# Gathers ahead of the histogram's end without waits, and a different mix of gathers and scatters

## The reference

```python
h = relu(layernorm(x))                        # over each row's 128 numbers
deg = segment_sum(1, src); deg_inv = rsqrt(deg) where deg > 0, else 0
norm = deg_inv[src] * deg_inv[dst]
msg[e] = alpha[type[e]] * norm[e] * sum_b comps[type[e], b] * (h[dst[e]] @ bases[b])
out = x + segment_sum(msg, src)               # 4 bases of 128 x 128
```

## Time and profile before

| | us |
|---|---|
| median of 3 runs | 767.62 (767.0 to 768.07) |
| profiled execution, time | 762.65 |
| profiled execution, span | 760.8 |
| POOL busy | 548.0 |
| DVE busy | 595.4 |
| PE busy | 565.7 |
| ACT busy | 368.6 |

### The profile page before, as it was taken

One profiled execution on the slowest core, in us unless ns is written; L12 is line 12 of the kernel. 1 busy time (PEld: TensorE's weight loads), 2 busy tenths in 40 slices (PEclk: granted clock), 3 DMA queues, 4 the chain that ended last, 5 costly groups with the idle time before them and its releaser, 6 DMA issues. The chain is left out here.

```text
span 760.8 us, 13653 instructions
## 1 busy us (share of the span) xinstructions
PE 565.7 (74%) x3922; PEld 396.5 (52%) x3922; DVE 595.4 (78%) x2624; ACT 368.6 (48%) x1494; POOL 548.0 (72%) x404
## 2 busy tenths in 40 slices
PE   1999995566576886659769778777889669788860
PEld 0766654344354664446556556555666446554430
DVE  4999995578577897749879899869998869896630
ACT  0144346245343565455646565644566546465530
POOL 1788886344237777877888888888888778777875
PEclk9999997988798999999989999989999989999995
DMA  3899989989944545344444445435444534444332
GB/s 116 293 353 350 321 306 336 315 276 349 317 131 91 94 98 103 54 85 89 95 81 98 95 80 96 96 54 117 76 79 94 112 63 96 78 71 73 35 36 24
DMA packets 56527, 108.89 MB, mean 143 GB/s; under 512 B 9291, under 2 KB 48216, under 8 KB 55636
## 3 DMA queue, kind: packets, MB, share of 16 engines
q0 software_dynamic: 34496, 25.72, 25.0%
q1 hardware_dynamic: 5372, 55.14, 20.0%
q10 hardware_dynamic: 16584, 27.16, 11.6%
HBM read 94.89 MB, written 64.61 MB: 210 GB/s over the span
## 5 line engine op out<-in xcount | busy, mean ns | idle before, releaser
L389 POOL DMA_INDIRECT out_dram<-acc,scatter_idx x196 | 313.2, 1598 | 97.2 <-issue 43.7
L368 POOL DMA_INDIRECT rows<-in_x_dram,dst_i x196 | 232.8, 1188 | 107.5 <-issue 39.0
L723 PE MATMUL pst<-table_bits,turned_hot 128*128 128x198 f16 x1568 | 177.0, 261 | 79.4 <-DVE masked L476 63.4
L742 PE MATMUL pst<-bases_sb,h_turned 128*128 128x512 f32 x392 | 211.6, 623 | 0.0
L723 PEld LDWEIGHTS pst<-table_bits,turned_hot 128*128 128x128 f16 x1568 | 143.1, 103 | 106.4 <-issue 50.6
L513 DVE SCALAR_TENSOR_TENSOR part_sum<-pst,coef,part_sum 128x128 f32<-128x128 f32 x392 | 115.9, 344 | 104.7 <-ACT part_sum L636 100.2
L750 PEld LDWEIGHTS pst<-rows,same 128*128 128x128 f32 x392 | 71.3, 197 | 184.0 <-issue 160.5
L476 DVE SCALAR_TENSOR_TENSOR masked<-iota_h,lo,pst 128x198 f32<-128x198 f16 x392 | 141.7, 416 | 15.9 <-PE pst L723 8.7
L636 ACT ACTIVATE part_sum<-pst,coef 128x128 f32<-128x128 f32 x196 | 71.1, 363 | 154.2 <-PE pst L742 114.3
L750 PE MATMUL pst<-rows,same 128*128 128x128 f32 x392 | 83.5, 296 | 72.8 <-ACT acc L646 69.9
L646 ACT ACTIVATE acc<-pst,sum_scale 128x128 f32<-128x128 f32 x196 | 71.5, 365 | 81.9 <-DMA out_dram<-acc,scatter_idx 56.3
(11 more groups left out here) (71 smaller groups left out, 413.6 us busy)
## 6 DMA issues: line engine op xcount, KB each, us to landing
out_dram<-in_x_dram SPq DMA_DIRECT2D x50, 1000.0 KB
src_row<-src_rows ACTq DMA_DIRECT2D x25, 512.0 KB
edge_row<-edge_rows ACTq DMA_DIRECT2D x45, 256.0 KB
rows<-in_x_dram,dst_i POOLq DMA_INDIRECT x196
out_dram<-acc,scatter_idx POOLq DMA_INDIRECT x196
rows<-edge_rows ACTq DMA_DIRECT2D x10, 175.0 KB
edge_row<-edge_rows SPq DMA_DIRECT2D x4, 256.0 KB
src_row<-src_rows SPq DMA_DIRECT2D x2, 512.0 KB
```

What stands on the lines that cost most here:

```text
L368: pool.indirect_dma_start(row(t), None, x, bass.IndirectOffsetOnAxis(ap=dst_i[:, t:t + 1], axis=0)) \
L389: pool.indirect_dma_start(out, bass.IndirectOffsetOnAxis(ap=scatter_idx[:, t:t + 1], axis=0), acc[:, t % ACC_RING, :], None, compute_op=AL ...
L723: last = pe.matmul(pst[:, LOOK + t % 2, k * LO:(k + 1) * LO], turned_hot[:, g % 2, c, k * W + j * P:k * W + (j + 1) * P], table[:, c * LO: ...
L742: pe.matmul(pst[:, PRODUCT + t % 4, :], h_turned[:, g % 2, j, :], bases_sb[:].rearrange("d b f -> d (b f)"), start=True, stop=True).then_i ...
```

## The change

`GATHER_RING` and its wait go; each of the 49 groups has a semaphore of its own. Of `pace` only the part for t below 56 stays. `FIRST_GATHERS` rises from 88 to 128, and in the scatter loop `gathers_until` gives one gather for two scatters, where it gave seven for ten. `stats_until` is not edited, but it calls `gathers_until`.

```diff
-    GATHER_RING = 8
-    HIST_GATHERS, LOOK_GATHERS, FIRST_GATHERS = 56, 64, 88
+    HIST_GATHERS, FIRST_GATHERS = 56, 128
     def gathers_until(t):
-        return min(TILES, FIRST_GATHERS + (7 * t + 9) // 10)
+        return min(TILES, FIRST_GATHERS + t // 2)
...
-        row_gathered = [sem(f"row_gathered{r}") for r in range(GATHER_RING)]
+        row_gathered = [sem(f"row_gathered{g}") for g in range(GROUPS)]
...
             def pace(t):
                 if 0 < t < HIST_GATHERS:
                     pool.wait_ge(hot_used, t * TILES // HIST_GATHERS)
-                elif HIST_GATHERS <= t < LOOK_GATHERS:
-                    pool.wait_ge(look_ps, ...)
-                elif LOOK_GATHERS <= t < FIRST_GATHERS:
-                    pool.wait_ge(product_ready, (t - LOOK_GATHERS) // 2 + 1)
             def gather(t):
                 g = t // GROUP
-                if t % GROUP == 0 and g >= GATHER_RING:
-                    pool.wait_ge(row_squared, g - GATHER_RING + 1)
                 pace(t)
...
-                    .then_inc(row_gathered[g % GATHER_RING], 16)
+                    .then_inc(row_gathered[g], 16)
...
             def stats(g):
-                act.wait_ge(row_gathered[g % GATHER_RING], 16 * GROUP * (g // GATHER_RING + 1))
+                act.wait_ge(row_gathered[g], 16 * GROUP)
```

More of the change, by code:

```diff
@@ L353, in pace @@
                     pool.wait_ge(hot_used, t * TILES // HIST_GATHERS)
-                elif HIST_GATHERS <= t < LOOK_GATHERS:
-                    pool.wait_ge(look_ps, (t - HIST_GATHERS + 1) * FIRST_LOOK * GROUP // (LOOK_GATHERS - HIST_GATHERS))
-                elif LOOK_GATHERS <= t < FIRST_GATHERS:
-                    pool.wait_ge(product_ready, (t - LOOK_GATHERS) // 2 + 1)
             def gather(t):
                 g = t // GROUP
-                if t % GROUP == 0 and g >= GATHER_RING:
-                    pool.wait_ge(row_squared, g - GATHER_RING + 1)
                 pace(t)
```

## The result

| | before | after |
|---|---|---|
| median, us | 767.31 (764.4 to 768.07, 4 runs) | 831.64 (825.72 to 833.66, 4 runs) |
| ratio | | 1.083 [1.077, 1.090] |
| profiled execution, time / span | 762.65 / 760.8 | 832.76 / 830.9 |

A forecast was written before the change was run, and what follows sets the result against it. POOL was taken to bound the loop, DVE next. Step 11 at 329, 29 steps of 10.7 us to 639 and 92 to the end give a 731.5 us span; with 1.85 and 5 added, 738, range 717 to 758.

The forecast's parts named there:

- No engine is made to wait.: Early gathers before the scatter loop: behind them is queued only the first scatter, which waits for the copies anyway; no cost.
- The end of the gathers: Early gathers on POOL: 72 at 1.27 us, 91 us in all, ending at 205 us, before the copies end.
- Rival C: Early gathers slow at 1.94 us each, ending at 254 us, where the scatters then start: 751 us; chance 0.16 with its like.
- D: Steps 1 to 4: look-up loads starve behind POOL's gathers, +32 us, 778 us in all, slower than before; chance 0.08.
- What they cost the copies: Stretch with DMA full: 40 more gathers, 2.6 MB, delay the copies by 8 us, bounds 0 and 19.
- S: Start of the scatter loop, set by the end of the copies: moves from 219.7 to 228 us.
- Steps 5 to 10: Two groups of statistics a step, DVE covering about 3 of 6.2 us: 13.4 us a step, 80 us by DVE's sum.
- Steps 11 to 40: Scatter loop: 29 steps of 10.7 us, 310 us, from 329 to 639, where 665.81 was.
- B: The forecast itself: DVE and the chain round it set the steps, 738 us, own range 730 to 746; chance 0.42.
- A: POOL still sets every step of the loop: -43 us, 725 us; chance 0.27.
- Step 40 to the end: Last stretch, bound by POOL's scatters as before: 92 us, where it was 95.

The follow-up runs named there:

- x9: The changed kernel a third time, unedited, in a job on chip 10: 830.05 us, 1.080 of the kernel before.
- x10: Changed kernel with gathers 56 to 127 waiting for look-ups and products, and ACT's statistics on the schedule of before: 746.23 us, 0.970 of the kernel before.
- x5: The changed kernel again, unedited, in another job on another chip: 743.58 us, 0.976 of the kernel before.
- x4: Changed kernel with 2 of the 50 copies of x to out, the other 48 left out: 733.9 us in one run.
- x14: Changed kernel without 48 of its 50 table copies, as x4, on another chip: 730.52 us.
- x17: Changed kernel without 48 of its 50 table copies, as x4, once more: 736.07 us in one run.
- x3: Changed kernel plus a watcher: ACT follows each of the first twelve look-ups with a small operation on DVE's semaphore: 736.0 us in one run.
- x12: Changed kernel with ACT's twelve watching operations, as x3, on another chip: 738.87 us, 0.969 of the kernel before.
- x16: Changed kernel with ACT's twelve watching operations, as x3, once more: 746.75 us in one run.
- x8: Changed kernel with ACT's statistics kept on the schedule of before: 727.71 us, 0.957 of the kernel before.
- x6: x3 again, the changed kernel with ACT's twelve watching operations: 745.26 us, 0.978 of the kernel before.
- x13: Changed kernel with three awaited small memsets on POOL between two of the early gathers: 765.04 us, 1.004 of the kernel before.
- x18: Changed kernel with three awaited small memsets between two early gathers, as x13, once more: 764.59 us in one run.
- x1: Changed kernel with waits back for gathers 56 to 127, on look-ups and then products: 741.46 us, 0.972 of the kernel before.

## Why the prediction was wrong, point by point

- **"No engine is made to wait."** This is the step that failed; the stretch before step 0, in which it put the cost at nothing, took 91.5 us more. I asked only what is queued behind the gathers on POOL. The waits that went also kept POOL's descriptors from running in one piece beside the first look-ups, and in two of six jobs the look-ups came up to 43 us late beside this piece. x9 and x10 show that the waits decide it on chip 10; for the first job that is taken over from there, and 10.9 of its 91.5 us were lost earlier, beside gathers that still waited for the histogram. The 1.26 us of a gather were right; what it did to others wasn't asked.
- **The end of the gathers**, forecast 205, came at 215.8 (215.5 in x5). The price was right, the start wrong: the sum counts 72 gathers from 113.9, where the kernel before is at its 50th; its 57th starts at 123.30.
- **Rival C and D** looked at the right stretch for other reasons. C's gathers beside DVE weren't slow: 0.95 us with DVE at work in x5 too. D's mechanism is there, but small. Steps 0 to 5 went from 105.6 us to 118.9 in x5, where I had allowed 2 us more, and D 32. In that stretch of x5 DVE waits for look-up loads (total, times, longest):

```profile
DVE turned_hot L463 <- DMA edge_row<-edge_rows: 9.5, 4, 3.2
```

  In the kernel before these waits are 0.4 us. In x4, x14 and x17, without copies, there are none and the steps take 104 to 107 us; in x3, x12 and x16, with them, 110 to 115. After and x9 reach these steps when the copies are over: no such wait, 107.2 and 105.6.
- **What they cost the copies**: 8 us, S at 228. In x5 the first scatter stands at 220.49, against 219.73 before: at most 1 us. In the stalled run SyncE's queue is done sooner than before:

```profile
23.06 177.63 SPq L309 DMA_DIRECT2D out_dram<-in_x_dram  x49
```

  at 200.7 against 212.9.
- **Steps 5 to 10**, 80 us by DVE's sum and 77 in the forecast, took 92.4 (91.7, 90.2 in x5, x9). The mechanism was named, two groups of statistics in one piece; its size was wrong. I took DVE's cover as 3 us of each 6.2, so that DVE waits 3 us a step; it waited 31.1 / 6 = 5.2. A step took 15.4 us; with at most one group, 11.7 (x8).
- **Steps 11 to 40**, forecast 310, took 304.0, 304.4 and 304.3: 10.5 us a step in place of 10.7. DVE was busy 284 of the 304 us, POOL 236 without its gaps. POOL by line, 435 to 740 us, against the earlier trace rows:

```profile
L382 POOL DMA_INDIRECT out_dram<-acc,scatter_idx x116 | 186.5, 1608 | 54.7 <-issue 27.5 <-DMA out_dram<-acc,scatter_idx 14.5 <-ACT acc L639 12.6
L361 POOL DMA_INDIRECT rows<-in_x_dram,dst_i x48 | 50.9, 1060 | 14.6 <-issue 13.1 <-ACT acc L639 0.9 <-DMA out_dram<-acc,scatter_idx 0.6
```

  The prices of a scatter and a gather haven't moved (1608 and 1060 ns), and POOL waits 13.5 us for sums, under the 20 to 40 that were to show B. That is between A and B.
- **Step 40 to the end**: 92 forecast, 91.1 measured.
- **Chance.** On the chips without stalls the span was 744.9 (x5) where 731.5 was forecast, 743.6 us as a time, inside the range. Part of that is luck: steps 0 to 11 took 27 us more than forecast, and a start 6.5 us sooner and steps 11 to 40 5.6 us shorter gave some of it back. A case in which the gathers hurt PE's or DVE's work itself wasn't among the rivals, at any price.

**What stays open.** Whether PE's raise of `look_ps` comes late or DVE is held: x3, x6, x12 and x16 were made for it and ran only where nothing stalls (in x3 ACT reaches its twelve operations at 130.82, when the last look-up's matmuls are done, so they tell nothing there). Three engines with "remote" waits in x10, and PE's gaps between matmuls that wait for nothing in the first job, speak for PE; that is argued, not shown. Whether the copies are needed for it (x4, x14, x17) and whether the rate of gathers or only their being unbroken counts (x13, x18) is open for the same reason, and so is what differs between the chips. That POOL's writing itself slows PE or its raises, or that both suffer from a third thing, can't be told apart either. The Trainium skill, "NOTIFIC — Programmer's Manual", section "2.4 When the ring fills", says of the block that writes trace records that a full queue can be set so that "the engine blocks until you make room". That would be a way for records to slow an engine; no run here shows it.

**The better version.** x8 beats both kernels on two chips (0.957 and 0.956), but has the unbroken row. x10 is the one that gained on a chip that stalls: 0.970 of the kernel before there, 84 us under the changed kernel. It didn't run elsewhere; x1, which shares its pace, was at 0.972 on a chip without stalls.

## What to carry to other kernels

A wait that costs its own engine nothing that matters can still do something: it breaks up a burst. Before taking such waits out, read the waits of other engines beside the burst for small entries that no instruction explains, since the 5.5 us of them in the kernel before became 88 (65.7 called remote, 22.0 called issue). When a function that sets a schedule is changed, follow each of its callers: `stats_until` cost 16 us. And run a change with a surprising result in several jobs, on several chips, before looking for its cause in the code.

## What the runs showed of the hardware

- The same program took 831.6, 743.6 and 830.1 us in three jobs, while the kernel before took 767.3, 760.9 and 766.8 in them. Within a job the runs of one kernel agree within 2%.
- On the two chips that stall, picks 8 and 9 start 40 to 44 us after the end of the matmuls that they need (42.9 and 41.2 in the first job, 43.5 and 40.3 in x9), a pick each 20 to 23 us, while POOL writes a gather each 1.26 us. The last long wait ends 7 to 8 us after the last gather.
- The price of writing a gather is the same in stalled and other runs: mostly 0.95 us beside the look-ups, and 0.30 us between two. Between scatters it is 1.06.
